# Attention rows of eight heads: spread by SP's transfers from DRAM in place of GpSimd's broadcasts

## What is computed

```python
def gat_conv(x, src, dst, W, a_src, a_dst, b, heads, out_ch):
    h = (x @ W).reshape(n, heads, out_ch)
    alpha_src = jnp.einsum('nhc,hc->nh', h, a_src)
    alpha_dst = jnp.einsum('nhc,hc->nh', h, a_dst)
    e = jax.nn.leaky_relu(alpha_src[src] + alpha_dst[dst], NEG_SLOPE)
    ...
    msg = h[src] * alpha[:, :, None]
    out = jax.ops.segment_sum(msg, dst, num_segments=n)
    return out.reshape(n, heads * out_ch) + b
```

## Time and profile before

| | us |
|---|---|
| runs (3): median, lowest to highest | 513.95, 513.72 to 514.45 |
| the profiled execution's own time | 513.88 |
| its span | 512.1 |
| TensorE busy | 468.3 (91%) |
| VectorE busy | 136.6 (27%) |
| ScalarE busy | 61.6 (12%) |
| GpSimd busy | 35.6 (7%) |
| DMA | 190.22 MB, mean 371 GB/s |

### The profile page before, as it was taken

One profiled execution on the slowest core, in us unless ns is written; L12 is line 12 of the kernel. 1 busy time (PEld: TensorE's weight loads), 2 busy tenths in 40 slices (PEclk: granted clock), 3 DMA queues, 4 the chain that ended last, 5 costly groups with the idle time before them and its releaser, 6 DMA issues.

```text
span 512.1 us, 6157 instructions
## 1 busy us (share of the span) xinstructions
PE 468.3 (91%) x2340; PEld 233.5 (46%) x2340; DVE 136.6 (27%) x361; ACT 61.6 (12%) x113; POOL 35.6 (7%) x53
## 2 busy tenths in 40 slices
PE   6999999999999999999999999897889789789881
PEld 5566665666568344344344353252243225224361
DVE  6564697437016311010010020010010002001166
ACT  0110212002003022020020110020020012002000
POOL 3432240000000301000000000000000000000000
PEclk9999999999999999999999999999999999999996
DMA  8999996876999699999999999999999999999800
GB/s 252 365 400 402 401 369 193 290 262 250 430 423 421 270 385 424 424 427 422 425 426 427 422 422 431 421 423 428 423 425 422 428 424 425 425 428 421 375 1 31
DMA packets 32571, 190.22 MB, mean 371 GB/s; under 512 B 5454, under 2 KB 5662, under 8 KB 18220
## 3 DMA queue, kind: packets, MB, share of 16 engines
q1 hardware_dynamic: 29260, 189.56, 91.2%
q10 hardware_dynamic: 2720, 0.41, 0.5%
q0 software_dynamic: 576, 0.06, 0.1%
HBM read 189.62 MB, written 0.39 MB: 371 GB/s over the span
## 4 chain that ended last, share of the span: by engine, by line
PE 58%; DMA 21%; SPq 12%; DVE 6%; issue 2%; ACT 1%; POOL 0%; DVEq 0%
DMA chunk<-in_L_ffn_W 13%; PE ps L1206 13%; PE ps L1233 13%; PE ps L1042 11%; PE ps L1002 10%; SPq L335 8%; DMA lower<-in_L_ffn_W 6%; SPq L330 3%; PE ps L1219 2%; PE ps L1180 2%; DMA slot<-in_L_gnn_W 2%; PE ps L1030 2%; PE ps L1057 2%; PE ps L972 1%; PE ps L1276 0%
## 5 line engine op out<-in xcount | busy, mean ns | idle before, releaser
L1206 PE MATMUL ps<-chunk,gathered 128*64 128x512 f32 x576 | 131.5, 598 | 17.6 <-DMA chunk<-in_L_ffn_W 17.4
L1233 PE MATMUL ps<-lower,hidden 128*64 128x384 f32 x768 | 131.8, 491 | 7.2 <-DMA lower<-in_L_ffn_W 7.2
L1233 PEld LDWEIGHTS ps<-lower,hidden 128*64 128x64 f32 x768 | 52.6, 136 | 72.7 <-issue 57.7
L1206 PEld LDWEIGHTS ps<-chunk,gathered 128*64 128x64 f32 x576 | 38.4, 136 | 98.8 <-issue 64.9
L1002 PE MATMUL ps<-slot,xT 128*128 128x384 f32 x192 | 64.4, 489 | 1.6 <-DMA slot<-in_L_gnn_W 1.6
L1042 PE MATMUL ps<-slot,eluT 128*128 128x384 f32 x168 | 55.3, 486 | 0.0
L829 DVE TENSOR_TENSOR biased<-ps,b_T 128x384 f32<-128x384 f32 x32 | 17.1, 555 | 135.3 <-PE ps L1219 135.3
L1002 PEld LDWEIGHTS ps<-slot,xT 128*128 128x128 f32 x192 | 35.5, 190 | 24.7 <-DMA slot<-in_L_gnn_W 2.6
L837 DVE TENSOR_SCALAR place_top<-slot_no,rank,small 128x128 f32<-128x128 f32 x8 | 4.0, 502 | 139.5 <-PE ps L1253 139.5
L1042 PEld LDWEIGHTS ps<-slot,eluT 128*128 128x128 f32 x168 | 31.5, 190 | 20.7
L497 ACT ACTIVATE hidden<-biased 128x384 f32<-128x384 f32 x32 | 16.3, 523 | 79.7 <-DVE biased L829 79.7
(11 more groups left out here) (278 smaller groups left out, 235.0 us busy)
## 6 DMA issues: line engine op xcount, KB each, us to landing
chunk<-in_L_ffn_W SPq DMA_DIRECT2D x48, 1536.0 KB, 28.9
lower<-in_L_ffn_W SPq DMA_DIRECT2D x64, 1152.0 KB, 30.0
slot<-in_L_gnn_W SPq DMA_DIRECT2D x31, 1152.0 KB, 13.7
slot<-in_L_gnn_W SPq DMA_DIRECT2D x3, 384.0 KB, 5.3
x_sb<-in_x SPq DMA_DIRECT2D x1, 384.0 KB, 3.6
out<-xc SPq DMA_DIRECT2D x1, 384.0 KB, 2.3
wv_half<-in_L_ffn_Wv ACTq DMA_DIRECT2D x2, 96.0 KB
b_rows<-in_L_ffn_b ACTq DMA_DIRECT2D x1, 96.0 KB
```

Source lines behind the costliest of these rows:

```text
L1206: last = T.matmul(ps[b * CAP:(b + 1) * CAP, s, 0:BANK], gathered[:, k, :], chunks[k][:, at:at + BANK], start=(k == 0), stop=(k == KT - 1))
L1233: last = T.matmul(ps[c * CAP:(c + 1) * CAP, 4, 0:HB], hidden[:, q, k, b, :], lowers[i][:, k, c * HB:(c + 1) * HB], start=(i == 0 and k == ...
```

## The change

SP now spreads the rows of all eight heads, of layer 2 and of its bias. `spread_rows(h)` issues two transfers of 384 KB. Each reads one row of 768 words in DRAM 128 times, once for each partition, into `att_rows`. From head 2 on SP waits first for `alpha_used`. The list `ATT_BEHIND` says behind which weight transfer n the pair of each head is issued. Behind n = 23 come three more for `att2_rows` and `gb2_rows`. VectorE waits for the landings (`att_in`, `att2_in`, `gb2_in`) in place of `spread`. GpSimd keeps the last two pairs, `wo_rows` and `wv_rows`, and its small arithmetic. The tensor `early_rows` goes.

```diff
+ATT_BEHIND = (2, 4, 11, 13, 15, 17, 19, 21)
...
+            def spread_rows(h):
+                if h >= 2:
+                    sp.wait_ge(alpha_used, h - 1)
+                for j, vectors in enumerate((gas1, gad1)):
+                    sp.dma_start(att_rows[:, h % 2, j, :],
+                                 vectors[h:h + 1, :].to_broadcast([P, D])).then_inc(att_in[h % 2], 16)
...
-                if n == 0:
-
-                    for j, vectors in enumerate((gas1, gad1)):
-                        sp.dma_start(early_rows[0:1, :, j, :], vectors[0:EARLY, :].unsqueeze(0)).then_inc(early_in, 16)
+                if n in ATT_BEHIND:
+                    spread_rows(ATT_BEHIND.index(n))
+                if n == 23:
+                    for j, vector in enumerate((gas2, gad2)):
+                        sp.dma_start(att2_rows[:, j, :], vector.to_broadcast([P, D])).then_inc(att2_in, 16)
+                    sp.dma_start(gb2_rows[:, 0, :], gb2.to_broadcast([P, D])).then_inc(gb2_in, 16)
...
-            pairs = [(gas1[h:h + 1, :], gad1[h:h + 1, :]) for h in range(HEADS)]
-            pairs += [(gas2, gad2), (gb2, gb2), (wo[0:1, :], wo[1:2, :]), (wv, bo)]
-            targets = [att2_rows, gb2_rows, wo_rows, wv_rows]
+            pairs = [(wo[0:1, :], wo[1:2, :]), (wv, bo)]
+            targets = [wo_rows, wv_rows]
...
-            for i in range(HEADS + 2):
-                spread_pair(i)
-
             pool.wait_ge(var_ready, 2)
             G.tensor_tensor(col(RSTD), col(VAR), half_pow[:, :], ALU.pow).then_inc(rstd_ready, 1)
-            spread_pair(HEADS + 2)
-            spread_pair(HEADS + 3)
+            spread_pair(0)
+            pool.wait_ge(spread, 1)
+            fetch(1)
+            spread_pair(1)
...
             def head_alpha(h):

                 dve.wait_ge(h_ready, h + 1)
-                dve.wait_ge(spread, h + 1)
+                dve.wait_ge(att_in[h % 2], 32 * (h // 2 + 1))
...
-            dve.wait_ge(spread, HEADS + 2)
+            dve.wait_ge(gb2_in, 16)
...
-            dve.wait_ge(spread, HEADS + 1)
+            dve.wait_ge(att2_in, 32)
```

More of the change, by code:

```diff
@@ L54 @@
 LOADS = CHUNKS + DOWN
-EARLY = 3
-ATONCE = 6
 WARM = (3, 5, 3, 4, 2, 2, 2, 6, 4, 4, 8, 20)
@@ L104, in gnn_moe_kernel @@
         x_sb = place("x_sb", [P, D])
-        src_hot, dst_hot, early_rows, eluT = region([
-            [("src_hot", [P, 8, P], bf16), ("dst_hot", [P, 8, P], bf16), ("early_rows", [1, 3, 2, D])],
+        src_hot, dst_hot, eluT = region([
+            [("src_hot", [P, 8, P], bf16), ("dst_hot", [P, 8, P], bf16)],
             [("eluT", [P, HEADS * KT, P])]])
@@ L228, in gnn_moe_kernel @@
         x_in, edges_in, small_in = sem("x_in"), sem("edges_in"), sem("small_in")
-        early_in = sem("early_in")
+        att_in = [sem("att_in0"), sem("att_in1")]
+        att2_in, gb2_in = sem("att2_in"), sem("gb2_in")
         row_in = sem("row_in")
@@ L359, in _, with fetch @@
             G.memset(half_pow[:, :], -0.5).then_inc(pool_ones, 1)
[L362 to L366, removed]
+            def fetch(i):
                 for j in range(2):
-                    pool.dma_start(places[i][:, j, :], pairs[i][j]).then_inc(landed, 16)
-            for i in range(EARLY, ATONCE):
-                fetch(i, row_in)
+                    pool.dma_start(rows[0:1, j, :], pairs[i][j]).then_inc(row_in, 16)
+            fetch(0)
             pool.wait_ge(var_ready, 1)
@@ L375, in _ @@
             G.tensor_tensor(col(RSTD), col(VAR), half_pow[:, :], ALU.pow).then_inc(rstd_ready, 1)
-            pool.wait_ge(early_in, 32)
             def spread_pair(i):
[L379 to L391, removed]
-            for i in range(HEADS + 2):
-                spread_pair(i)
+                pool.wait_ge(row_in, 32 * (i + 1))
+                G.partition_broadcast(targets[i][:, :, :].rearrange("p a c -> p (a c)"),
+                                      rows[0:1, :, :].rearrange("p a c -> p (a c)")).then_inc(spread, 1)
             pool.wait_ge(var_ready, 2)
             G.tensor_tensor(col(RSTD), col(VAR), half_pow[:, :], ALU.pow).then_inc(rstd_ready, 1)
-            spread_pair(HEADS + 2)
-            spread_pair(HEADS + 3)
-            pool.wait_ge(spread, len(pairs))
+            spread_pair(0)
+            pool.wait_ge(spread, 1)
+            fetch(1)
+            spread_pair(1)
+            pool.wait_ge(spread, 2)
             G.memset(cf_w[:, 0:2, :], 0.0).then_inc(cf_init, 1)
@@ L514, in _ @@
             round_(0, first=True)
-            act.wait_ge(spread, HEADS + 4)
+            act.wait_ge(spread, 2)
             act.wait_ge(minus_ready, 1)
@@ L853, in _ @@
                 round_(r)
-            dve.wait_ge(spread, HEADS + 4)
+            dve.wait_ge(spread, 2)
             V.tensor_tensor_reduce(out=blocks(xc[:, :]), in0=ps[:, 6:8, 0:HB], in1=blocks(wv_rows[:, 0, :]),
```

## The result

| | before | after |
|---|---|---|
| median of the runs (lowest to highest), us | 513.93 (513.72 to 514.45, 4 runs) | 527.65 (526.53 to 528.09, 4 runs) |
| the profiled execution's own time, us | 513.88 | 526.53 |
| its span, us | 512.1 | 524.7 |

The ratio is 1.0255, with a 95% interval of 1.0239 to 1.0272. The forecast of 526.9 us was right in time and in mechanism. The profiled execution of the changed kernel is the fastest of its four: the medians differ by 13.7 us, the profiled executions by 12.65. No trace shows the other three executions, so that 1.1 us is not explained.

The account below looks back on a forecast made before the run. TensorE was taken to bound the graph layers and DMA the experts, so early TensorE delay reaches the end. 513.9 + 13.8 (late rows) + 1.4 (clock) - 2.2 (broadcasts gone) = 526.9 us, range 523 to 535.

Parts of the forecast that it names:

- Lateness of head 3's rows: Graph layers: head 3's pair lands behind SP's backlog at 58.9 us, scores start at 61.1 instead of 47.27; +13.8 us.
- Clock: TensorE idles about 12 us before the scores, its clock falls and work resumes at half speed; +1.4 us (0 to 3).
- Broadcasts gone: Ten of twelve GpSimd broadcasts go, so VectorE is no longer held from 66 us on; -2.2 us (-2.5 to -1.5).
- Costed at nothing: Late early slots, pairs of heads 4 to 7, layer-2 and bias rows: hidden or in time, 0 us.
- Volume: Rival: DMA bounds everywhere, so the added 7.5 MB cost their whole 17.7 us; 531.6 us, chance 0.08.
- Dear rows: Rival: 128 reads of one DRAM row collide, a pair costs 3.4 us, scores +19.6; 532.7 us, chance 0.11.
- lone latency: Rival: each row transfer pays its own 3.6 us, 7.2 a pair, scores at 82.1; 547.9 us, chance 0.03.
- The rule of a fixed 2.0 us for each transfer: Skill's fit: 2.9 us per 384 KB transfer, head 3's rows landing at 74.3; about 542 us.
- Rows in time: Rival: head 3's pair lands before its head is ready at 44.08 us, leaving only the gain; 511.7 us, chance 0.06.
- One sign: Expected evidence on SP's queue: `att_rows` transfers take some 20 us from issue to landing; 5 us would show it wrong.

Follow-up runs that it names:

- early_rows_later: Kernel before, with SP's two small transfers for `early_rows` issued behind n = 1 instead of n = 0; 513.39 us, ratio 0.9983.
- warm_gap: The change plus 105 dummy matmuls on TensorE ahead of the scores of heads 0 to 3; 536.81 us, ratio 1.0434.
- gpsimd_later: Kernel before, with GpSimd's broadcast of head 7's pair and those behind it held until VectorE's eighth elu input; 511.86 us, ratio 0.9943.
- early_pairs: The change with pairs of heads 2 and 3 in borrowed buffers, issued behind n = 6 and n = 8 without a wait; 524.02 us, ratio 1.019.
- four_buffers: The change with four row buffers in turn and pairs behind n = 2, 5, 6, 8, 12, 13, 15, 18; 518.99 us, ratio 1.0084.
- four_buffers_bias_up: As the change with four row buffers and re-placed pairs, but bias rows moved from behind n = 23 to n = 17; 511.84 us, ratio 0.9954.
- later_both: Kernel before, with head 7's broadcast and those behind it held later and the `early_rows` transfers behind n = 1; 511.16 us, ratio 0.994.
- two_slots_up: The change with pairs of heads 2 and 3 behind n = 10 and n = 11 instead of 11 and 13; 522.25 us, ratio 1.0151.
- warm_gap_short: The change plus 44 dummy matmuls on TensorE ahead of the scores of heads 0 to 3; 525.99 us, ratio 1.0216.

## Why the prediction was right

**Lateness of head 3's rows: +13.8 predicted, +13.18 measured** (60.45 - 47.27). The chain was as worked out: backlog, landing, two dots, scores. The pair's price was exact (a landing is an issue's start and its time to landing): in the change the two transfers of head 2 land at 48.10 + 1.96 = 50.06 us, and those of head 3 at 56.21 + 1.96 = 58.17, each at once behind the slot before them. The 0.7 us too much came from the queue's head. The two transfers for `early_rows` had stood there, and without them n = 1 landed at 12.14 us instead of 13.19. The prediction had removed them at no price. early_rows_later, where n = 1 lands at 12.79, confirms the sign, not the size. The slots from n = 1 to n = 13 took 0.3 us more than before, which gave a part of it back.

**Clock: +1.4 predicted, +1.64 measured.** In the change the granted clock was 0.50 of full (the 1.2 GHz level) from 53.5 to 63.5 us; warm_gap and the kernel before give the same stretch at full clock as 1.64 us shorter.

**Broadcasts gone: -2.2 predicted, -2.18 measured.** From n = 12 to n = 15 the runs start 15.98 us apart (76.38 to 92.36), where it was 18.16. gpsimd_later, which keeps the broadcasts and only moves them, has n = 15 earlier by 1.97 us; its ratio, 0.42 to 0.72% less, is 2.2 to 3.7 us.

The sum of the three is 12.64 us, the span grew by 12.6; the forecast's own sum was 13.0. That the median of 527.65 us is also near 526.9 is partly luck: it lies 1.1 us above the profiled execution, for a reason that no term names.

**Costed at nothing.** The late slots did stop TensorE, 1.02 us at n = 5, and the wait for head 3 swallowed it. Where nothing swallows it, this term isn't small: 2.10 us and 1.7 more at half clock in early_pairs. The pairs of heads 4 to 7 landed at 65.98, 74.02, 82.03 and 89.77 us, in time. The bias rows landed at 99.71 instead of near 98 and held VectorE for 0.47 us, which cost TensorE nothing. These margins were thin: with the lateness of head 3 removed, they became stalls of 6.08 us (early_pairs) and 5.42 us (four_buffers).

**The rivals.** Volume fell with four_buffers_bias_up, which moves 7.5 MB more than later_both and takes 0.7 us more, not 17.7. Dear rows and lone latency fell with the pair's 1.96 us. The rule of a fixed 2.0 us for each transfer (the Trainium skill, "DMA: Bandwidth & Descriptors", "Anatomy of one DMA") would have made it an estimated 5.8, and no room for a fixed part shows between transfers on a full queue. Rows in time would have needed a queue without a backlog. One sign was wrong: from issue to landing I had written some 20 us, and it was 13.6 to 14.6. SP was held at one issue after the other (up to 7.09 us at a slot, 2.77 at a row) and came to head 3's pair only at 41.72 us, so the landing, worked out from bytes ahead, came out and the latency didn't.

## What to carry to other kernels

A transfer that joins a full queue lands when all bytes ahead of it have landed, so work out its landing from the bytes and put it where it lands ahead of its reader; its own bytes may cost next to nothing (here 7.5 MB, at most 0.7 us) and its place several microseconds (here 7.2 for one transfer of 384 KB). When a stall is removed, list every later item of that queue with its new due time first: twice here the next one took much of the gain back.

## What was not expected of the hardware

Short stalls of TensorE were followed by a lower clock. After 2.10 us of waiting its granted clock was 0.57 in the mean of the next 4 us, and a run that takes 4.14 us took 5.80; after 1.91 us (two_slots_up) the run took 5.83, while after 1.02 us in the change it took 4.14:

```profile
30.46 4.14 PE L993 MATMUL ps<-slot,xT 128*128 128x384 f32 x12 [1.02 <-DMA slot<-in_L_gnn_W]
```

After 3.10 us (warm_gap_short), behind 10 us of dummies, the clock fell 0.8 us after work had resumed. A stall of 2 us thus cost up to 1.7 us more than itself. And 4.55 us of standing (two_slots_up) cost as much in clock as 12.26: from the scores to the turning it took 10.40 us, against 10.28 in the change.

128 reads of one 3 KB row in DRAM, one for each partition, ran at the full rate (384 KB in 0.98 us, half of 1.96).
